# A state-space mixer, two mixtures of experts and an attention in one kernel: norms, residuals and weight loads moved across the three stage borders

## The reference

```python
x = x + mixer(ctx, layernorm(x))      # conv of 4 taps, SiLU, B/C/delta projections, softplus,
                                      # state[n] = state[n]*exp(delta*A[n]) + delta*u*B[n], 16 states,
                                      # y = sum_n state[n]*C[n] + D*u, times silu(layernorm(x)) as gate
x = x + ffn0(layernorm(x))            # shared SwiGLU (704 wide) times sigmoid(x @ Wsg)
                                      # + 8 experts of 176, softmax router, top 2
x = x + attention(layernorm(x), ctx)  # 16 heads of 128, keys and values from ctx, RMS-normed q and k
x = x + ffn1(layernorm(x))            # shared SwiGLU (352 wide) + 16 experts of 176, 4 groups,
                                      # best 2 groups, top 4
```

## Time and profile before

| | |
|---|---|
| three runs | 862.51, 863.74, 867.19 us (median 863.74) |
| profiled execution | 862.79 us, span 860.5 us |
| PE matmul busy | 775.7 us (90%) |
| PE weight load busy | 634.2 us (74%) |
| DVE / ACT / POOL busy | 551.9 / 425.5 / 392.9 us |
| granted PE clock, mean | 0.97 |

### The profile page before, as it was taken

The page is one execution under the profiler, slowest core; times in us unless marked ns, Lnnn a source line. Parts: engine busy times, 40 slices in busy tenths (PEclk is TensorE's granted clock), DMA queues, the critical chain, the costliest instruction groups (busy, mean ns, idle before and its releaser), DMA issues. The chain is left out here.

```text
span 860.5 us, 12977 instructions
## 1 busy us (share of the span) xinstructions
PE 775.7 (90%) x4358; PEld 634.2 (74%) x4358; DVE 551.9 (64%) x935; ACT 425.5 (49%) x861; POOL 392.9 (46%) x299
## 2 busy tenths in 40 slices
PE   8475766899999986999999999999879999999997
PEld 3122222588888865889899898998758888888886
DVE  4999999553333363788888888888867433333333
ACT  2763434553434333666666666666634434343442
POOL 1499761356556533332323323222034565565653
PEclk9689999899999997999999999999989999999999
DMA  3422000112333221011010110000011533333331
GB/s 107 198 98 98 0 0 1 56 39 76 114 104 110 85 99 37 1 38 38 2 37 0 37 37 0 0 0 1 1 38 40 149 109 110 104 110 110 107 121 52
DMA packets 17808, 52.93 MB, mean 62 GB/s; under 512 B 2986, under 2 KB 5619, under 8 KB 16756
## 3 DMA queue, kind: packets, MB, share of 16 engines
q1 hardware_dynamic: 17506, 52.04, 19.1%
q10 hardware_dynamic: 274, 0.53, 0.2%
HBM read 51.35 MB, written 1.21 MB: 61 GB/s over the span
## 5 line engine op out<-in xcount | busy, mean ns | idle before, releaser
L1041 DVE TENSOR_TENSOR f_su<-f_sg,psum 128x512 f32<-128x512 f32 x84 | 57.7, 687 | 198.1 <-PE psum L87 180.2
L938 POOL TENSOR_TENSOR f_h_lo<-f_hid,f_h_hi 128x512 fp32r<-128x512 f32 x84 | 108.7, 1295 | 117.6 <-ACT f_h_hi L924 112.5
L85 PE MATMUL psum<-xT_hi,f_gu_hi 128*128 128x512 f32 x336 | 133.1, 396 | 4.2 <-DVE xT_lo L675 3.2
L86 PE MATMUL psum<-xT_lo,f_gu_hi 128*128 128x512 f32 x336 | 132.2, 393 | 0.0
L87 PE MATMUL psum<-xT_hi,f_gu_lo 128*128 128x512 f32 x336 | 131.5, 391 | 0.0
L924 ACT ACTIVATE f_h_hi<-f_hid 128x512 fp32r<-128x512 f32 x84 | 53.1, 632 | 157.1 <-DVE f_hid L1053 157.1
L85 PE MATMUL psum<-f_dn_hi,f_h_hi 128*128 128x256 f32 x336 | 94.8, 282 | 1.5 <-POOL f_h_lo L938 1.5
L1420 POOL TENSOR_TENSOR a_rr<-a_ss,eps 128x8 f32<-128x8 f32 x32 | 6.4, 200 | 195.5 <-DVE a_ss L1459 195.5
L87 PE MATMUL psum<-f_dn_hi,f_h_lo 128*128 128x256 f32 x336 | 95.1, 283 | 0.0
L86 PE MATMUL psum<-f_dn_lo,f_h_hi 128*128 128x256 f32 x336 | 95.0, 283 | 0.0
L441 POOL TENSOR_TENSOR m_dbu<-m_du,m_b_all 128x1024 f32<-128x1024 f32 x32 | 74.9, 2350 | 36.7 <-DVE m_du L517 21.5
(11 more groups left out here) (208 smaller groups left out, 1889.4 us busy)
## 6 DMA issues: line engine op xcount, KB each, us to landing
f_raw<-in_moe SPq DMA_DIRECT2D x42, 384.0 KB, 3.0
m_b_all<-b_rows SPq DMA_DIRECT2D x8, 1024.0 KB, 4.9
f_comb<-scratch SPq DMA_DIRECT2D x30, 256.0 KB, 3.8
a_raw<-in_w_pair SPq DMA_DIRECT2D x8, 768.0 KB, 4.4
f_comb<-scratch SPq DMA_DIRECT2D x6, 448.0 KB, 3.4
f_comb<-scratch SPq DMA_DIRECT2D x6, 384.0 KB, 3.4
f_comb<-scratch SPq DMA_DIRECT2D x6, 320.0 KB, 3.5
f_comb<-scratch SPq DMA_DIRECT2D x6, 192.0 KB, 3.8
```

What stands on the lines that cost most here:

```text
L85: pe.matmul(out, a[0], b[0], start=first, stop=False, skip_group_check=True)
L86: pe.matmul(out, a[0], b[1], start=False, stop=False, skip_group_check=True)
L938: return pool.tensor_tensor(out, whole, hi, ALU.subtract)
L1041: dve.tensor_tensor(su[:, hs, :], sg[:, hs, :], up_bank(half), ALU.mult).then_inc(su_s, 1)
```

## The change

The same arithmetic, in another order and with other buffers.

- **Mixer.** The layer norm of x (statistics, rstd, shift) goes ahead of the state loop. The gate of half 0 (`gate(0)`, ACT, with a table load before and one after), `gated_out`, `turned` and `residual` of half 0, the statistics, the scaling (now on ACT) and the transposes, high and low parts of the next norm's half 0 go into steps 17 to 31 of the state loop. The weights of the first two expert chunks are split there too. Twelve more matmuls of zeros stand ahead of the first convolution; the load of `sel` moves from ACT's queue behind x on SP's.
- **Half 1 of the mixer's end** (`rest`) is done inside the block of experts 0, behind its first `gate_up`.
- **Experts.** All steps are written out in an order of (chunk, half) (`ORDER0`, `ORDER1`): experts 0 starts with half 0 of four chunks and ends with half 1 of four. The split weights have a ring of six. Half 1 of the norm is done at steps 0 to 2. In the last steps of experts 0: residual, statistics and scaling of half 0, its transposes, the first weights of attention.
- **Attention.** All units are written out. It starts with q and k of unit 0 from half 0 alone; the residual and the norm of half 1 run beside it. In its last units: statistics of half 0, the first two expert chunks, and in the end step the scaling and the transposes.
- Buffers are laid over each other so that all of this fits. The twelve matmuls of zeros at the start of each later block are gone.

The core of the diff:

```diff
@@ mixer, tensor
+                keep_warm(pe, sh, 5, 12)
...
                     added(k)
-                for b in range(B):
-                    pe.wait_ge(yz_ready, b // 2 + 1)
-                    turned(b)
+                    if k == DS + 4:
+                        pe.wait_ge(pre_kept, 1)
+                        turned(pe, 0)
+                    if k == DS + 6:
+                        pe.wait_ge(x_new, 1)
+                        turned(pe, 1)
+                    if k == DS + 12:
+                        norm_turned(pe, sh, after, 0, 0, TURN)
+                    if k == DS + 14:
+                        pe.wait_ge(after.hi, 1)
+                        pe.wait_ge(after.full, 1)
+                        pe.wait_ge(after.lo, 1)
+                        norm_turned(pe, sh, after, 0, 1, TURN)
@@ mixer, scalar
+                    if k == DS + 1:
+                        gate(0)
+                        act.preload_act_table_set("natural_log_exp_and_others")
                     if k == DS + 2:
                         act.wait_ge(y_added, DS)
...
+                    if k in (DS + 4, DS + 6):
+                        sh.weights.gate_up_high(act, (k - DS) // 2 - 2)
+                        sh.weights.down_high(act, (k - DS) // 2 - 2)
+                    if k == DS + 12:
+                        act.wait_ge(after.rstd, 1)
...
+                    if k == DS + 14:
+                        norm_hi(act, sh, after, 0, 0, TURN, sh.xT_full)
+                norm_hi(act, sh, after, 0, 1, TURN, sh.xT_full)
+                gate(1)
@@ mixer, vector
                     weighted(k)
-                    if k == 8:
-                        dve.wait_ge(ln_rstd, 1)
-                        dve.scalar_tensor_tensor(nmr[:, :], mv[:, :, 0], -1.0, rstd[:, :], ALU.mult, ALU.mult).then_inc(ln_step, 1)
...
+                    if k == DS + 3:
+                        gated_out(dve, 0)
+                    if k == DS + 5:
+                        residual(dve, 0)
+                    if k == DS + 7:
+                        residual(dve, 1)
+                    if k == DS + 8:
                         dve.wait_ge(x_new, 2)
                         norm_statistics(dve, sh, after, 0)
+                    if k == DS + 13:
+                        norm_lo(dve, sh, after, 0, 0, TURN)
+                norm_lo(dve, sh, after, 0, 1, TURN)
@@ experts, tensor
-                norm_tensor(pe, sh, s)
...
                 pe.wait_ge(s.lo, KD)
                 pe.wait_ge(s.full, KD)
-                gate_up(0, 0, 0)
-                pe.wait_ge(s.lo, 2 * KD)
+                gate_up(J0)
+                rest.tensor(pe)
...
+                    down(j)
+                    if after is not None and j == J1 - 2:
+                        for k in range(KD):
+                            norm_turned(pe, sh, after, 0, k, NEXT[k])
@@ experts, vector
-                norm_vector(dve, sh, s)
...
+                rest.vector(dve)
+                norm_statistics(dve, sh, s, 1)
...
+                    if after is not None and j == J1 - 3:
+                        residual(0)
+                        dve.wait_ge(mix.x_back, 2)
                         norm_statistics(dve, sh, after, 0)
+                    if after is not None and j == J1 - 2:
+                        norm_scaled(dve, sh, after, 0)
@@ attention, tensor
-                norm_tensor(pe, sh, s)
...
-                project(0, (1,))
-                project(1, (1,), FIRST)
-                pe.wait_ge(s.lo, 2 * KD)
-                project(0, (0,)).then_inc(qk_ps, 1)
-                project(1, (0,), FIRST).then_inc(qk_ps, 1)
+                project(0, (1,), FIRST)
+                pe.wait_ge(s.lo, KD)
+                project(0, (0,), FIRST).then_inc(qk_ps, 1)
+                pe.wait_ge(moe[0].x_back, 4)
+                project(1, (1, 0)).then_inc(qk_ps, 1)
+                for h, out in enumerate((OT, OUT)):
+                    norm_turned(pe, sh, s, 1, h, out)
```

More of the change, by code:

```diff
@@ L612, in __init__ @@
             self.full = sem("full")
+        self.read = self.full if routed else self.hi
 def norm_statistics(dve, sh, s, h):
@@ L679, with norm_scaled @@
-GU = 2 * KD * P
-WCH = GU + DM
-HS = 4
-def moe_block(nc, sh, tag, s, after, weights, router, scratch, experts, shared, groups, gated, out):
-    NC = chunks_of(experts, shared)
-    NU = 2 * NC
-    SC = shared_chunks(shared)
-    ER = experts + (1 if gated else 0)
-    SP = -(-SC // 2)
-    assert NC % 2 == 1 and SC >= 3
+def norm_scaled(dve, sh, s, h):
+    dve.wait_ge(s.rstd, h + 1)
+    if h == 1:
+        dve.wait_ge(s.turned, KD)
+    for n in range(TPH):
+        t = h * TPH + n
+        dve.tensor_scalar(sh.xn[:, n, :], sh.x[:, t, :], sh.mv[:, t, 0:1], sh.rstd[:, t:t + 1],
+                          ALU.subtract, ALU.mult).then_inc(s.normed, 1)
@@ new lines, in norm_turned, with norm_hi @@
+def norm_turned(pe, sh, s, h, k, out):
+    pe.wait_ge(s.normed, (h + 1) * TPH)
+    for n in range(TPH):
+        mm = pe.transpose(out[:, n * P:(n + 1) * P], sh.xn[:, n, k * P:(k + 1) * P], sh.ident[:, :])
+    mm.then_inc(s.turned, 1)
+def norm_hi(act, sh, s, h, k, out, full=None):
+    tok = slice(h * HALF, (h + 1) * HALF)
+    act.wait_ge(s.turned, KD * h + k + 1)
+    act.activation(sh.xT_hi[:, k, tok], out, ACT.Copy).then_inc(s.hi, 1)
+    if full is not None:
+        act.activation(full[:, k, tok], out, ACT.Copy).then_inc(s.full, 1)
@@ new lines, in moe_block @@
+def moe_block(nc, sh, mix, rest, after, pre, out):
+    m, s, w = mix.m, mix.norm, sh.weights
+    experts, groups, gated, wr = mix.experts, mix.groups, mix.gated, mix.wr
+    C0 = 0 if m == 0 else NC0
+    SC = shared_chunks(mix.shared)
+    J0, J1 = START[m], STOP[m]
+    steps = range(J0, J1)
+    prefetched = (C0, C0 + 1)
+    beside = {j: [c for c in range(C0 + 2, C0 + (NC0, NC1)[m]) if prepared(c) == j] for j in range(J0 - 1, J1)}
+    first_routed = min(j for j in steps if STEPS[j][0] >= C0 + SC)
+    half_done = max(j for j in steps if STEPS[j][1] == 0)
+    TURN_AT, HIGH_AT, LOGITS_AT, ROUTE_AT, PICK_AT, SPREAD_AT = (
+        (1, 2, 2, 3, 5, 6), (0, 1, 1, 2, 3, 4))[m]
@@ L1083 @@
+                if after is not None:
+                    for k in range(KD):
+                        norm_lo(dve, sh, after, 0, k, NEXT[k])
+                if out is not None:
+                    for h in range(2):
+                        residual(h)
 QK = (KD + 1) * HP * HD
@@ L1289, in step @@
                         output(n - 1)
+                        if end:
+                            for h, out in enumerate((QT, KT)):
+                                norm_turned(pe, sh, after, 0, h, out)
                         if (n - 1) % B == 1 and not (static and t > NUA - B):
```

959 lines of the change are left out of this document (533 added, 426 removed).

## The result

The changed kernel takes 858.16 us (median of 12 runs, 854.45 to 860.13) against 864.75 for the kernel before, timed beside it. The ratio is 0.9907, with a 95% interval of 0.9885 to 0.9929. So it is faster, by 0.9% and not by the 1.8% of the forecast, and the time lies 1.2 us above the range. It was the fastest of the twelve, 3.7 under their median.

The account below looks back on a forecast made before the run. DVE was taken to bound the state loop, PE the experts and attention, short-step chains the borders. Terms -2.0 + 8.0 - 10.8 + 4.4 - 10.0 - 3.8 = -14.2 took span 860.5 to 846.3; plus 2.3, 848.6, written 848.0 (838 to 857).

Parts of the forecast that it names:

- the term for experts 1: Experts 1: eight transposes 1.0, small waits 0.7, an old wait of 0.3 gone, half the low-clock loss; +0.7 us.
- The first half of the change gives almost nothing: Start through experts 0: the terms nearly cancel, so experts 0 ends at 311.6 us.
- The border to attention: Experts 0 to the first scores: 24.7 us shrinks to 14.7 at most, -10.0 us (-12 to -7).
- the start: Start of the mixer: earlier first scan, `nmr` ahead of the loop, twelve more zero matmuls; -2.0 us (-2.9 to +2.4).
- the last border: Attention to experts 1: 9.20 us becomes 4.0, -5.2.
- Experts 0: Experts 0: added turns and transposes on PE, and waits, less an old stall; +4.4 us (3.0 to 8).
- The gate fitted between two steps: State loop, ACT: `gate(0)` with two table loads and decays takes 7.2 us and just fits, 0.3 to spare.
- Rival 4: All three long stages: straight code costs PE time per added instruction; 869 us at 0.01 us each; chance 0.05.
- State loop: State loop, second half: half 0's work between scans on DVE adds its whole time; +8.0 us (5.2 to 12).
- So no wait: State loop residuals: turned values come 2 steps later, 6.7 us, against PE sums of 1.88 and turns of 1.09.
- First border: State loop's end to experts 0's first `gate_up`: 18.4 us becomes 7.65, -10.8 us.
- case 2: Borders: additions are covered and PE's clock might stay at 2.4 GHz; -6, giving 842 us; chance 0.08.

Follow-up runs that it names:

- before_straight: The kernel before, with only attention's loop of three times eight units written out on all engines: 865.50 us, ratio 1.0002.
- quiet_gate: The changed kernel with POOL held idle while DVE does the gated output of half 0 in the state loop: 850.21 us, ratio 0.9796.
- exp1_scale: The changed kernel with the scaling of half 1 ahead of the first `f_hid` on DVE in experts 1: 854.97 us, ratio 0.9877.
- late0: The changed kernel with all of the mixer's half 0 work back behind the last step of the state loop: 858.43 us, ratio 0.9913.
- pool_gate: The changed kernel with the gated output of half 0 on POOL in place of DVE: 852.07 us, ratio 0.9842.

## Why the prediction was wrong

The forecast of 848.0 stands 10.2 us under the median. Of these, 6.4 are in the span of the profiled execution (846.3 forecast, 852.7 measured), and 3.7 lie between that execution and the median. The step that failed most is the term for experts 1, "small waits (0.7)" and a low-clock loss cut by half: +0.7 forecast, +6.0 measured.

**What held.** The sign and the main mechanism: the borders shrank by 26 us, and the stages between took much of it back. "The first half of the change gives almost nothing" was put too well: experts 0 was to end at 311.6 after 312.0 before, and ended at 315.7, so the whole gain is from the second half. The border to attention (-11.4 for -10.0), the start and the last border came within their bounds. Experts 0 (+4.7 for +4.4) is right in part by luck. The wait for the third chunk's low part was there (1.17 for 1.2), but the 1.0 for the split weights was not, and a stretch of low clock at the stage's start (0.57 over 3.38 us, 1.5 lost) was in no term. Attention's -0.7 for +0.7 also comes of the clock, as shown above. The gate fitted between two steps with its loads at 1.28 each and no gap on either side, and no scan waited for the decays behind them. The Trainium skill, page "ScalarE: Activation LUTs", section "What ACT_TABLE_LOAD costs", has a drain of about 1.38 us at each switch, which would have made these decays late; the changed kernel's trace does not show it either. Rival 4's mechanism, PE's own instructions slower in straight code, was not seen in attention: what before_straight shows is 0.1 us more of waiting for DVE in most units. In the experts a steady unit, in which PE never waits, takes 4.187 for 4.180; that is under the rival's 4.20, and its cause was not tested. Of the sums, the terms of experts 0 add to 4.5 and not 4.4, and those of the border to attention to 14.5 at most and not 14.7; neither matters.

**State loop, +1.5.** The gated output was taken at 2.6 from a neighbouring row and measured 3.24, 2.0 of it contention with POOL, as quiet_gate shows. "So no wait" for the residual was wrong: the working took PE's sums at 1.88, the higher clock, while PE's clock in this loop was 0.91 and 0.50 at that step; the wait was 1.02. The statistics came cheaper (1.8 for 2.3) and the low part too (1.7 for 1.9); some 0.5 is in no single row.

**First border, +2.0: an error of the working.** The old border was counted from the last product but one (142.96, 18.4 us), the new one from the last product, so the step between the two, 1.8 us, was taken as gained. Counted from the last product in both, the same sum gives -9.0, and -8.8 was measured.

**Experts 1, +5.3: the term that was mis-sized.** PE's waits in the stage were 1.94, 1.17, 0.77 and 0.37, 4.25 in all for the 1.37 of before, which had the like of the last two (0.73 and 0.37). So +2.9 stands where the term had 0.7 less 0.3. I had followed PE's list at this border and not DVE's, where half 1's scaling stood behind an `f_hid`. The wait also brought a second low-clock stretch of 1.7, where the term had half a stretch less: 2.5 together. exp1_scale puts 3.4 of the 5.3 down to this one order. The steady units (4.187 for 4.180) add some 0.3 over 50 units.

**The last 3.7 us.** The median of the changed kernel lies that much above its profiled execution. Half a clock for 6.8 us costs 3.4 us, and such a stretch stood at the router of experts 0 in four variants with unchanged experts, and not in the profiled execution of the changed kernel. That its slower executions had one is the likely reading. Seven of the twelve took 858.05 to 860.13 us at a mean granted clock of 0.966 to 0.968, the other five 854.45 to 856.01 at 0.968 to 0.972, and a stretch of 6.8 us at half the clock takes 0.004 off that mean. None of the slower ones was profiled, so it is not shown. Of the clock, the range had only what it does at the borders (case 2), and left out a fall inside a full stage.

## What to carry to other kernels

Work moved off a border into a stage that its engine already fills is paid there in full: by late0, 9.3 us in the loop for 9.2 at the border. It pays only on an engine with room, which for the gated output was POOL. Read the list of every engine in the first steps behind a border, above all where a wait is a few us and its cause a neighbour's order of two instructions. And count both ends of a border from the same instruction.

## What the runs showed of the hardware

A DVE instruction with both operands in SBUF (128x512, float32) took 1.2 and 2.2 us beside POOL instructions (3.32 the pair, changed kernel) and 0.68 with POOL idle (quiet_gate); the same pair on POOL took 2.5 (pool_gate). PE's granted clock fell to 1.2 GHz for 3.4 or 6.8 us behind 32 narrow matmuls in one piece (outputs 8 or 16 columns wide) in 14 of 21 places, though PE was busy before, during and after, and in none of the 7 places where they stood between wide ones. Table loads took 1.28 us with no time ahead of or behind them (88.67 and 92.06 in the changed kernel). Attention's loop written out cost 0.84 us in 280, in waits between engines (before_straight).
